# Sixteen sets of four heads in a cross-attention kernel: loops on each engine, or written out in a row

## What is computed

```python
x = x + xattn(layernorm(x), ctx_768, Wq, Wk, Wv, Wo, bo)   # 4 batches, 256 rows, 4096 keys, 16 heads of 64
x = x + attn(layernorm(x), ...)                            # recurrence over 256 rows, 16 heads of 16
x = x + ffn(layernorm(x), ...)                             # 8 experts, the best 2 of each row, and a shared one

def xattn(x, context, Wq, Wk, Wv, Wo, bo):
    q, k, v = heads(x @ Wq), heads(context @ Wk), heads(context @ Wv)
    attn = softmax(einsum('bhid,bhjd->bhij', q, k) * 64 ** -0.5)
    return merge(einsum('bhij,bhjd->bhid', attn, v)) @ Wo + bo
```

## Time and profile before

| | us |
|---|---|
| median of 3 executions (2289.08 to 2293.04) | 2289.66 |
| the profiled execution's own time | 2283.85 |
| its span, first to last instruction | 2281.9 |
| start of quad 0 / of quad 15 (row_max, L338) | 85.4 / 1737.2 |
| mean granted TensorE clock, share of full speed | 0.979 |

### The profile page before, as it was taken

One profiled execution on the slowest core, in us unless ns is written; L12 is line 12 of the kernel. 1 busy time (PEld: TensorE's weight loads), 2 busy tenths in 40 slices (PEclk: granted clock), 3 DMA queues, 4 the chain that ended last, 5 costly groups with the idle time before them and its releaser, 6 DMA issues. The chain is left out here.

```text
span 2281.9 us, 51658 instructions
## 1 busy us (share of the span) xinstructions
PE 2070.4 (91%) x19834; PEld 1532.7 (67%) x19834; DVE 1498.0 (66%) x1760; ACT 1320.5 (58%) x1593; POOL 1430.9 (63%) x652
## 2 busy tenths in 40 slices
PE   4799999999999999999999999999999778666998
PEld 3577777767777777777777767777777543225787
DVE  5666666766666667666666666666666337995685
ACT  2476767676767667666767676767676541002432
POOL 0377767766777777766777767777777722552454
PEclk9899999999999999999999999999999889997999
DMA  8010101110110112010100120101000030000320
GB/s 229 15 34 14 27 14 41 48 37 14 27 28 13 28 27 72 14 27 14 29 16 24 34 66 15 34 6 34 7 24 4 3 124 0 0 0 10 117 97 37
DMA packets 44682, 80.08 MB, mean 35 GB/s; under 512 B 7073, under 2 KB 31265, under 8 KB 43697
## 3 DMA queue, kind: packets, MB, share of 16 engines
q1 hardware_dynamic: 44464, 76.80, 11.8%
HBM read 70.03 MB, written 5.31 MB: 33 GB/s over the span
## 5 line engine op out<-in xcount | busy, mean ns | idle before, releaser
L761 POOL TENSOR_TENSOR acc<-acc,PR 128x1024 f32<-128x1024 f32 x480 | 1156.0, 2408 | 362.3 <-ACT PR L542 340.8
L617 DVE TENSOR_REDUCE amx<-ps 128x2 f32<-128x1024 f32 x512 | 626.6, 1224 | 467.2 <-PE ps L317 466.7
L542 ACT ACTIVATE PR<-ps 128x1024 f32<-128x1024 f32 x512 | 518.7, 1019 | 246.9 <-PE ps L325 246.9
L502 ACT ACTIVATE ps<-NM 128x1024 f32<-128x1024 f32 x416 | 427.1, 1028 | 200.5 <-DVE V L602 154.6
L333 PE MATMUL ps<-PR,V 128*64 128x256 f32 x4096 | 504.5, 389 | 0.1
L333 PEld LDWEIGHTS ps<-PR,V 128*64 128x64 f32 x4096 | 273.5, 138 | 162.7 <-issue 32.8
L325 PE MATMUL ps<-qh,KH 64*128 64x256 f32 x2048 | 333.4, 319 | 31.6 <-ACT ps L502 27.6
L300 PE MATMUL ps<-wv,C 64*128 64x256 f32 x4608 | 314.5, 280 | 0.6
L300 PEld LDWEIGHTS ps<-wv,C 64*128 64x128 f32 x4608 | 304.9, 187 | 10.2 <-issue 2.0
L289 PE MATMUL ps<-C,wk 64*128 64x512 f32 x2304 | 308.4, 395 | 0.8 <-DVE x L651 0.4
L325 PEld LDWEIGHTS ps<-qh,KH 64*128 64x128 f32 x2048 | 196.4, 185 | 163.0 <-issue 81.6
(11 more groups left out here) (168 smaller groups left out, 1860.3 us busy)
## 6 DMA issues: line engine op xcount, KB each, us to landing
wk<-wk_split SPq DMA_DIRECT2D x62, 192.0 KB, 3.2
wv<-wv_split SPq DMA_DIRECT2D x30, 384.0 KB, 5.0
bc<-wm_rows SPq DMA_DIRECT2D x16, 512.0 KB, 4.8
craw<-in_ctx SPq DMA_DIRECT2D x30, 256.0 KB, 3.9
we<-in_we SPq DMA_DIRECT2D x8, 768.0 KB, 6.9
wo<-in_wo SPq DMA_DIRECT2D x68, 64.0 KB, 2.1
wq<-in_wq SPq DMA_DIRECT2D x32, 128.0 KB, 2.7
craw<-in_ctx SPq DMA_DIRECT2D x30, 128.0 KB, 3.8
```

Source lines behind the costliest of these rows:

```text
L502: act.activation(ps[:, first_bank:first_bank + 2, :].rearrange("p h (k n) -> p h k n", k=2), row.unsqueeze(2).to_broadcast([P, 2, 2, ROWS] ...
L542: act.activation(PR[:, pr_slot(t, hf), :, :, :].rearrange("p h k n -> p (h k n)"), ps[:, bank:bank + 2, :].rearrange("p h n -> p (h n)"), ...
L617: dve.tensor_reduce(amx[:, :, t, c], psG, AX.X, ALU.max).then_inc(g_max, 1)
L761: pool.tensor_tensor(flat(acc[:, :, :, :]), flat(acc[:, :, :, :]), flat(PR[:, pr_slot(t, hf), :, :, :]), ALU.add).then_inc(acc_done, 1)
```

## The change

The function `loops` no longer makes hardware loops. It calls `quad` sixteen times with Python numbers, so that each engine gets sixteen copies of the quad's code in a row, with constants in the waits and in the DMA addresses. The flags of each quad, and the order of the work within it, are as before. The other hunks drop the argument `eng`.

```diff
@@ -130,15 +130,11 @@
         def has_job(t, final):
             return not (final and t >= NEXT_QUAD)
 
-        def loops(eng, quad):
-            if nb > 1:
-                with eng.Fori(0, nb - 1) as b:
-                    with eng.Fori(0, NG - 1) as g:
-                        quad(b * NG + g, b, g, False, False)
-                    quad(b * NG + (NG - 1), b, NG - 1, True, False)
-            with eng.Fori(0, NG - 1) as g:
-                quad(g + (nb - 1) * NG, nb - 1, g, False, False)
-            quad(nb * NG - 1, nb - 1, NG - 1, False, True)
+        def loops(quad):
+
+            for it in range(nb * NG):
+                b, g = it // NG, it % NG
+                quad(it, b, g, g == NG - 1 and b < nb - 1, it == nb * NG - 1)
 
         def wait_drained(eng, it, t, side):
 
...
-            loops(sp, quad)
+            loops(quad)
...
-            loops(pe, quad)
+            loops(quad)
...
-            loops(act, quad)
+            loops(quad)
...
-            loops(dve, quad)
+            loops(quad)
...
-            loops(pool, quad)
+            loops(quad)
```

## The result

The kernel after takes 2255.82 us (median of 4 executions, 2254.74 to 2260.31), the kernel before, on the same chip, 2289.37 (4 executions, 2280.80 to 2293.04). The ratio is 0.9862, 95% interval 0.9832 to 0.9893: 1.4% faster. Forecast were 2262.0 with a range of 2252 to 2273. The profiled execution of after took 2260.31, with a span of 2258.3, against 2283.85 and 2281.9 before. So the medians differ by 33.5 us and the profiled executions by 23.5; the prediction said 27.4. Executions of one kernel spread over some 0.5% here, and the longer ones profiled show a lower granted TensorE clock.

The account below looks back on a forecast made before the run. PE's matmul stream was taken as the bound within a quad, with savings at the seams. 18.9 + 1.3 + 3.0 + 4.2 = 27.4 us off the profiled 2283.85, plus 5.8 to the median, gave 2262 us; range 2252 to 2273.

Parts of the forecast that it names:

- Part 1: Ten seams between quads entered by PE's taken jump: the jumps go, saving 18.9 us.
- part 2: Four seams where the loop falls through: they lose loop and wait register work, saving 1.3 us.
- the sample: Seam into quad 15, already outside loops with constants in waits: 9.37 us, expected for all fifteen seams.
- The dear seam: Seam of 13.12 us, clock 0.87, right behind a jump's stall; expected to become like the others.
- Part 3: Change of pair inside a quad, step 7 to 8: 0.2 us each in fifteen quads, 3.0 us; range 0 to 5.1.
- Part 4: Ordinary steps, 210 in fifteen quads: fewer PE register instructions save 0.02 us a step, 4.2 us.
- Part 5: ACT table loads, 8 us lost at eight seams if they stayed; SP's refresh-chain register work, put at 0, up to 1.5.
- The refills of the small engines: ACT and DVE run dry at each new instruction page: 60 us of refills if uncovered, 2323 us; 5 in 100.
- Every handoff quicker: One PE handoff in each of 210 steps gains half of 0.22 us: 23 us more, 2243 us; 6 in 100.
- No change: PE's 3.6 us are a refill due to code length, staying once per turn elsewhere: about 2288 us; 3 in 100.

Follow-up runs that it names:

- eleven-turn loop: The changed kernel plus a PE loop of eleven turns around a satisfied wait, at the ten quads formerly entered by a taken jump: 2276.75 us, ratio 0.9960.
- outer-loop kernel: The kernel before with one hardware loop over three batches, four quads written out in it, and the last batch written out behind it: 2271.68 us, ratio 0.9925.
- two near copies: Kernel before with each quad in a one-turn hardware loop, 2255.38 us (0.9849); changed kernel with a two-turn PE wait loop heading each quad, 2256.34 us (0.9856).

## Why the prediction held, and where it did not

**Part 1, the jumps, and part 2, the seams that fall through: right.** 20.2 us were expected, 19.2 came. Writing out removed the standstill, nothing took its place, and the seams became nearly those of the sample. The sample was a seam too cheap by 0.06 us (9.37, where all came out at about 9.43), fifteen times over: that is the missing 1.0. Its own seam had grown to 9.42 too, and this repeats: 9.34 to 9.37 in five traces with loops on PE, 9.40 to 9.45 in the nine without one there. PE waits 0.39 us for DVE's division there, with constants, as the timeline of after shows, where I had read 0.33 from the earlier trace rows:

```profile
1715.15 1.13 PE L344 MATMUL ps<-wo,Otn 128*128 128x256 f32 x4 [0.39 <-DVE Otn L641]
```

The mechanism of the dear seam was right as well: the clock fell behind a standstill, which the eleven-turn loop repeats. The explanation of part 2 was right too, in what it said of the waits: from the end of the division to `project_out` it takes 0.27 us at all four seams that fell through, and 0.05 into quad 15 and at every seam of after. That is 0.21 of the 0.34 between 9.71 and 9.37; of the rest, 0.11 lies behind `project_out` (5.92 us to the seam's end against 5.81). The loop's own register work, which part 2 also named, costs nothing that a seam shows.

**Part 3, the change of pair: wrong.** 3.0 us were expected, nothing came. The failed step is "I take 0.2, as the 0.22 in the idle of the earlier trace rows", and with it the assumption that what the handoff saves reaches the end. Timelines of the place (start, duration, idle before), before and then after:

```profile
249.79 1.27 POOL L765 TENSOR_TENSOR accf<-acc 128x512 f32<-128x512 f32 x1
...
250.28 1.06 DVE L645 TENSOR_TENSOR Otn<-Ou,Otn 128x256 f32<-128x256 f32 x1
...
251.49 0.69 PE L348 MATMUL ps<-wo,Otn 128*128 128x256 f32 x2 [0.51 <-DVE Otn L645]
```

```profile
248.71 1.27 POOL L761 TENSOR_TENSOR accf<-acc 128x512 f32<-128x512 f32 x1
...
249.11 1.14 DVE L641 TENSOR_TENSOR Otn<-Ou,Otn 128x256 f32<-128x256 f32 x1
...
250.31 0.92 PE L344 MATMUL ps<-wo,Otn 128*128 128x256 f32 x3 [0.51 <-DVE Otn L641]
```

The handoff did become quicker: from the division's end (251.34 and 250.25) to the start of `project_out` it takes 0.15 us before and 0.06 after. That is 0.09 and not 0.2, since at this place one register instruction carries the wait and no second follows it, as one does at a seam. And the 0.09 was taken back ahead of the division. POOL's fold (the sum of the accumulator's halves) starts 2.06 us after the window's start before (247.73) and 2.15 after (246.56), and the division ends 1.55 us after the fold's start in both, whether it takes 1.06 or 1.14. In the fourteen traces, refresh quads and quad 15 aside, it ends 1.54 to 1.56 us after the start of the fold, although it starts 0.07 to 0.51 behind it and takes 1.05 to 1.48: the later it starts, the shorter it is. At a seam the fold starts 0.06 later too (1.96 before quad 15, 2.02 in after), which is what the sample missed. That the fold sets the end of the division is read from these rows; no run changes the fold to show it.

**Part 4, the ordinary steps: right in kind, a little too large.** Of the 4.2 us expected in fifteen quads 3.4 fall to the twelve ordinary ones, which gained 2.8; by the outer-loop kernel it is 0.26 in a quad's fifteen steps, 0.017 a step where I took 0.02. In this cut the quads include their change of pair.

**Part 5: the table loads went, and cost nothing; the refresh chain was worth more than nothing.** I put SP's register work in it at 0, with up to 1.5 us. The refresh quads gained 2.7 in one pair of traces and 4.9 in the other. Some 0.8 of it is the steps of part 4, and in the second pair a clock of 0.98 in all three quads before, against two after, adds to it. All engines but PE written out gave 310.2 with two quads below full clock, as before had, so the gain is theirs; which of them has it is open. A link of the chain lost 0.36 us; I had named the chain, and priced it without reading SP's rows in it. This miss and that of part 3 nearly cancel. The sum of 27.4 stands 3.8 above the trace (23.6) also because head and tail were 2.1 longer and quad 15 was 1.0 shorter, all of which I had put at nothing.

**The distance between profile and median.** I kept the 5.8 us that before's median stood above its profile. After's median stands 4.5 below its own. Before's executions reach from 2280.8 to 2293.0 in this measurement, and the execution profiled at 2283.85 was one of its short ones; the one at 2290.97 has its 7 us from stretches at a lower clock. The medians differ by 33 to 34 us in three comparisons (ratios of after 0.9862, and 0.9849 and 0.9856 of its two near copies) and by 26.6 in one (0.9895). The granted clock of single executions tells how much of this is the change. Before's times go with it, from 2295 us at a mean clock of 0.971 to 2273 at 0.983, in 61 executions. The ten of after, at 0.974 to 0.980, lie 20 to 29 us below the straight line through those 61, 25 in the mean. So my estimate is 25 us at an equal clock, a little under the 27.4 of the sum. That the median of after fell to 2255.8, 6 us below the forecast, where the sum was too large, is the luck of a few executions.

**The rivals.** The refills of the small engines (2323): none to be seen. Their queue has 48 packets where I had guessed 100, steps 0 to 4 of a late quad take 26.11 as those of the first (26.10), and with all engines but PE written out the time fell. Every handoff quicker (2243): no, 0.017 us a step. No change: no, there is nothing in the place of the jumps.

## What to carry to other kernels

Where a hardware loop's body on TensorE is large, look in the trace for its taken branch: if it takes microseconds, compare a seam with a jump to one without and take that difference as the price of each turn, since part of the branch lies beside queued matmuls. Registers in waits and branches to near targets are worth almost nothing on an engine that has work queued. They count where the engine is idle for the wait: look for register instructions between the end of the work waited for and the start of the work that waits (0.27 us here against 0.05). Addresses computed between DMA issues lengthen a chain link by link (0.36 us here); whether somebody gains by a shorter link has to be read at an equal clock. An idle at a handoff does not shrink by what the handoff saves if a third engine sets when the work ahead of it ends.

## What the runs showed of the hardware

- A compare-and-branch on PE took 67 to 86 ns not taken, 0.21 us taken over a few instructions, and 3.3 to 3.9 us taken to the start of a quad's code, with one 16 KB instruction packet fetched meanwhile. The Trainium skill (Advanced Engine Details and Errata, Control Flow Timing) gives about 108 ns for it. The first kind lies somewhat below that (34 to 67 ns on the other engines, taken or not), the others far above.
- Behind a standstill of PE of 3.3 to 4.0 us the clock dropped from 2.4 to 1.2 GHz for a stretch at none to three of the ten seams of a trace, at 1.5 to 1.9 us each. In the three traces of before it was each time the seam 3 to 4, and once 7 to 8 as well.
- Outside the refresh quads, DVE's division (128x256) beside POOL's fold (128x512, 1.27 us) ended 1.54 to 1.56 us after the fold's start, whether it started 0.07 or 0.51 behind it.
- Three 512-column matmuls more in the later steps of quad 15 did not raise its mean clock (0.91, then 0.92).
- One DMA over 128 partitions whose source has an outer dimension of two, in place of two over 64, made the longest wait for a context chunk 17.5 us instead of 5.3, with 0.14 of the DMA engines busy in a window of the transfer instead of 0.77.
